# A two-layer LSTM + RNN on one core: one matmul unit of every step moved behind the second layer's recurrent product

## The reference

```python
xW = jnp.einsum('ntd,dk->tnk', x, Wx) + b            # layer 0, 4 gates x 512
def step(carry, xw_t):
    prev_h, prev_c = carry
    a = xw_t + prev_h @ Wh
    i, f, o = sigmoid(a[:, :H]), sigmoid(a[:, H:2*H]), sigmoid(a[:, 2*H:3*H])
    g = tanh(a[:, 3*H:])
    next_c = f * prev_c + i * g
    next_h = o * tanh(next_c)
x = x + hs_of_layer0                                  # then layer 1 on this x
def step1(h, xw_t): return tanh(h @ Wh1 + xw_t)       # xW1 = x @ Wx1 + b1
x = x + hs_of_layer1
```

## Time and profile before

| | before |
|---|---|
| median of 3 runs | 2181.52 us |
| profiled execution, time / span | 2183.09 / 2181.0 us |
| TensorE matmul (PE) busy | 2158.0 us, 99% |
| TensorE weight load (PEld) busy | 1779.9 us, 82% |
| VectorE (DVE) / ScalarE (ACT) busy | 2097.6 us, 96% / 1696.9 us, 78% |
| GpSimd (POOL) busy | 113.9 us, 5% |
| mean granted TensorE clock | 0.998 |

### The profile page before, as it was taken

The page is one execution under the profiler, slowest core; times in us unless marked ns, Lnnn a source line. Parts: engine busy times, 40 slices in busy tenths (PEclk is TensorE's granted clock), DMA queues, the critical chain, the costliest instruction groups (busy, mean ns, idle before and its releaser), DMA issues.

```text
span 2181.0 us, 148256 instructions
## 1 busy us (share of the span) xinstructions
PE 2158.0 (99%) x63856; PEld 1779.9 (82%) x63856; DVE 2097.6 (96%) x11013; ACT 1696.9 (78%) x5916; POOL 113.9 (5%) x165
## 2 busy tenths in 40 slices
PE   7999999999999999999999999999999999999998
PEld 4888888888888888888888888888888888888886
DVE  7999999999999999999999999999999999999998
ACT  5777777777777777777777777777777777777775
POOL 0220000000000000000000000000000000000000
PEclk9999999999999999999999999999999999999999
DMA  5000000000000000000000000000000000000000
GB/s 220 19 14 19 23 24 19 14 19 24 24 18 24 14 19 24 24 19 14 18 24 24 19 24 14 19 24 24 19 14 22 21 24 19 24 14 19 24 14 13
DMA packets 17259, 53.88 MB, mean 25 GB/s; under 512 B 1888, under 2 KB 3040, under 8 KB 15328
## 3 DMA queue, kind: packets, MB, share of 16 engines
q1 hardware_dynamic: 15792, 43.85, 5.6%
q10 hardware_dynamic: 816, 0.56, 0.1%
HBM read 27.62 MB, written 16.78 MB: 20 GB/s over the span
## 4 chain that ended last, share of the span: by engine, by line
PE 97%; DVE 2%; ACT 0%; DMA 0%; issue 0%; ACTq 0%; DVEq 0%
PE in_ps L273 25%; PE rec_first_ps L273 21%; PE rnn_ps L273 20%; PE rec_second_ps L273 20%; PE c_ps L273 11%; DVE largest_slice L503 0%; DMA b_sb<-b 0%; DVE wh_part L555 0%; DVE turned L599 0%; PE in_ps L442 0%; ACT wh_part L802 0%; DVE uv L627 0%; DVE h_parts L653 0%; DVE pre_sb L607 0%; DVE gates_cell L632 0%
## 5 line engine op out<-in xcount | busy, mean ns | idle before, releaser
L273 PE MATMUL rec_first_ps<-wh_part,h_parts 128*32 128x256 f16 x16352 | 544.6, 273 | 2.7 <-DVE h_parts L653 2.2
L273 PE MATMUL rec_second_ps<-wh_part,h_parts 128*32 128x256 f16 x16320 | 543.0, 273 | 2.0 <-DVE wh_part L555 2.0
L273 PEld LDWEIGHTS rec_second_ps<-wh_part,h_parts 128*32 128x32 f16 x16320 | 453.0, 97 | 2.4 <-ACT rec_second_ps L813 2.2
L273 PEld LDWEIGHTS rec_first_ps<-wh_part,h_parts 128*32 128x32 f16 x16352 | 380.0, 95 | 83.9 <-issue 7.4
L273 PE MATMUL in_ps<-wx_sums,x_sums 128*32 128x256 f32 x5760 | 379.7, 379 | 0.0
L838 ACT ACTIVATE gates_cell<-gate_ps,unscale 128x128 f32<-128x128 f32 x511 | 187.6, 367 | 208.6 <-DVE gate_ps L607 208.5
L273 PE MATMUL rnn_ps<-wh_parts,h_parts 128*32 128x256 f16 x8096 | 318.0, 273 | 4.7 <-DVE h_parts L692 4.7
L273 PE MATMUL rnn_ps<-wx_sb,y 128*32 128x128 f32 x8192 | 321.3, 273 | 0.4 <-ACT rnn_ps L825 0.4
L273 PEld LDWEIGHTS rnn_ps<-wx_sb,y 128*32 128x32 f32 x8192 | 252.3, 110 | 80.2 <-ACT rnn_ps L825 0.9
L825 ACT ACTIVATE rnn_ps<-rnn_ps,mask_scaled 128x256 f32<-128x256 f32 x506 | 225.2, 445 | 76.8 <-DVE turned L669 61.7
L273 PEld LDWEIGHTS in_ps<-wx_sums,x_sums 128*32 128x32 f32 x5760 | 195.7, 110 | 92.8
(11 more groups left out here) (116 smaller groups left out, 3386.5 us busy)
## 6 DMA issues: line engine op xcount, KB each, us to landing
yT<-y SPq DMA_DIRECT2D x64, 256.0 KB, 2.4
x_sb<-xT SPq DMA_DIRECT2D x31, 512.0 KB, 4.1
wh_sb<-wh SPq DMA_DIRECT2D x5, 1024.0 KB, 10.3
wx_sb<-wx SPq DMA_DIRECT2D x5, 1024.0 KB, 17.9
b_sb<-b ACTq DMA_DIRECT2D x1, 256.0 KB, 6.0
x_sb<-xT ACTq DMA_DIRECT2D x1, 256.0 KB, 17.8
x_sb<-xT SPq DMA_DIRECT2D x1, 256.0 KB, 21.8
b_sb<-b SPq DMA_DIRECT2D x1, 64.0 KB, 21.4
```

The costliest lines, as they stand in the source:

```text
L273: last = nc.tensor.matmul(out[QUAD * q:QUAD * (q + 1)], states, weights(q), start=False, stop=True, tile_position=(0, QUAD * q), skip_grou ...
```

## The change

The last unit of each step is taken out of its place between `recurrent0` and `input1` and issued at the end of the step, behind `recurrent1`. Its `slot_done` goes with it. Steps without `units` (t below 27) are as before.

```diff
-            def units(g, first, end):
+            def units(g, first, end, last_of_slot):
...
-                last.then_inc(slot_done, 1)
+                if last_of_slot:
+                    last.then_inc(slot_done, 1)
...
                         elif g >= PLAIN:
-                            units(g, UNITS_OF_PART[part], UNITS_OF_PART[part + 1])
+                            units(g, UNITS_OF_PART[part], UNITS_OF_PART[part + 1] - 1, False)
...
                     recurrent1(s)
                     if STEPS - 1 <= t < STEPS + LAG - 1:
                         keep_busy(in0_ps[0], BUSY_GROUPS[t - STEPS + 1])
+                if t < SLOTS:
+                    g, part = divmod(t + 5, SPAN)
+                    if g >= PLAIN:
+                        units(g, UNITS_OF_PART[part + 1] - 1, UNITS_OF_PART[part + 1], True)
```

## The result

| | before | after |
|---|---|---|
| median, 6 runs each | 2181.83 us | 2217.66 us |
| ratio, with 95% interval | | 1.0159 (1.0149 to 1.017) |
| span of the profiled execution | 2181.0 us | 2215.8 us |
| PE / DVE / ACT busy | 2158.0 / 2097.6 / 1696.9 | 2190.7 / 2116.0 / 1695.6 us |
| mean granted TensorE clock | 0.998 | 1.0 |

Forecast were 2205.5 us, 24 more than before; measured are 35.8 more. Lines behind line 368 have moved down by up to 5: L653 is now L658, L692 is L697, L813 is L818, L615 is L620, L787 is L792, L599 is L604.

The account below looks back on a forecast made before the run. TensorE's work (4.13 us) and the loop through VectorE (4.15) were taken to bound each step together. The terms 19.2 + 3.6 + 1.2 = 24 us gave 2205.5 us; likeliest range 2196 to 2222, 8-in-10 range 2192 to 2236.

Parts of the forecast that it names:

- Both engines stand at the limit, so any lateness shows: Per step, TensorE's work (4.13 us) and the loop through VectorE (4.15) are nearly equal; lateness on either shows in full.
- A wait at `recurrent1` of 0.05 behind L692, 4.19 a step: TensorE reaches `recurrent1` earlier and waits for L692: 0.04 over 4.15 in 480 steps, 19.2 us.
- The 0.14 that I kept as a far bound: Gap from L653 to `rec_first_ps`; if it held at `recurrent1`, 0.13 a step, 62 us.
- ScalarE's first seed at R + 0.25: R is the step's start at `rec_first_ps`; ScalarE's first L813 waits for the moved unit and starts 0.55 us later.
- `rec_second_ps` just fits: Seeded by R + 0.68 to 0.71, load at R + 0.77: cost 0; rival of late seeds 2253 us, chance 0.15.
- Part 1, 0 to 0.07, taken 0.03: Units needing ScalarE's L787 start 0.03 to 0.12 late, so `recurrent1` is late: 0.03 in 120 steps, 3.6 us.
- Part 0, 0.01: ScalarE's gates start up to 0.26 late, mostly taken up before L692 and L653: 0.01 x 120, 1.2 us.
- Parts 2 and 3: 0: ScalarE has longer idle times ahead of the gates there, so its later start costs 0.
- the likeliest case's range: 2196 to 2222 us, for 14 to 41 us added; the case has chance 0.70.
- the wide range: 2192 to 2236 us, to hold 8 times in 10; top: half of ScalarE's rival price or the way's far bound.
- the 48: Price of the rival that ScalarE's queue pays: 0.1 us in 480 steps, 2253 us; chance 0.15.
- Clock: Rival: TensorE's pauses in each step lower its clock; one step in ten at half clock, 198 us, 2404; chance 0.01.

Follow-up runs that it names:

- f6: The kernel before, but the first matmul of `recurrent0` no longer makes its redundant wait for `seed0_done[0]` (t = 5 to 507); 2170.51 us, ratio 0.9943.
- e2: The changed kernel, but the last unit is moved behind `recurrent1` in parts 2 and 3 alone; 2192.52 us, ratio 1.0045 to before.
- e3: The changed kernel, but ScalarE waits for the moved unit only where it reads it, part 2 keeping the early wait; 2205.84 us, ratio 1.0108 to before.
- e8: As e3, but part 1 issues its first unit last and part 2's early wait for `slot_done` goes too; 2200.32 us, ratio 1.0084 to before.
- f4: The changed kernel, but the last two units of each step stand behind `recurrent1` instead of one; 2409.39 us, ratio 1.1038 to before.
- f9: e8 with the same redundant `seed0_done[0]` wait removed as in f6; 2196.62 us, ratio 1.0058 to before.
- f5: The kernel before with every unit in its old place, but `slot_done` signalled later, by one of `recurrent1`'s last four matmuls; 2197.06 us, ratio 1.0061.
- e1: The changed kernel, but each step's last unit stands behind `input1` and ahead of `recurrent1`; 2181.29 us, ratio 0.9997 to before.

## Why the prediction was right, and what it mis-sized

- *Both engines stand at the limit, so any lateness shows.* Right. Steps are 4.15 before, and f6 shows that the loop through L653 held them 0.02 above TensorE's own 4.13.
- *A wait at `recurrent1` of 0.05 behind L692, 4.19 a step.* Right in kind and place. In every kernel in which TensorE waits there the median is 0.05 (after in parts 0, 2 and 3, e2, e3, e8, f4, f9); the step is 4.180, so 0.03 a step (15 us) rather than 0.04 (19), and the 0.01 taken for weights that could not be loaded ahead did not come. e8 isolates it: 14 us by its medians, 18 by its time. The 0.14 that I kept as a far bound belongs to a first matmul whose load waits behind a separate semaphore instruction, which this wait does not have: f6 takes that instruction away, and its load comes 0.06 us sooner behind VectorE.
- *ScalarE's first seed at R + 0.25.* Right: 0.25 in part 0, 0.27 in part 2.
- *`rec_second_ps` just fits.* Right; this rival did not come: in parts 0 and 3 the second L604 starts 1.97 to 1.98 into the step (median), as L599 did in before (1.98).
- *Part 1, 0 to 0.07, taken 0.03.* The range held, the value was too low: 0.057 over parts 0 and 3 (7 us instead of 3.6), because the way from L792 to the units is 0.10 where 0.05 to 0.14 was allowed. e3 shows it: with the copies early, the extra is gone.
- *Part 0, 0.01.* It is 0.
- *Parts 2 and 3: 0.* This is the step that failed. Part 3 is 0. In part 2 I looked only at ScalarE's idle time ahead of the gates, and not at who waits for the seed itself: L615 on VectorE does, and it lies in the loop that sets the step. Part 2 pays 0.078 over parts 0 and 3, 9 us; e3 against e8 shows it (0.061 a group, and gone when the early wait is gone), and f5 has it without the move.
- The sum by terms: 15 + 7 + 9 = 31 us by the medians, against 24 forecast. Some 4 us more are in longer steps that I had no term for. That 2217.66 still lies in the likeliest case's range, 2196 to 2222, is in part luck: its high end has room for a wait of 0.06 a step and for 0.03 in part 0, which did not come, and none for part 2, which did. The far end of the wide range, 2236, does not follow from the prices named for it either: half of the 48 gives 2229.5, the far bound of 62 gives 2243.5.
- *Clock.* It did not fall: 1.0 (2.4 GHz) in the profiled execution and 0.998 to 1.0 in the five others, though TensorE pauses in every step; in f4, with a pause of 0.3 us a step, it was 0.999.

## What to carry to other kernels

In a loop where two engines are both full, put behind a waiting instruction nothing that could have stood ahead of it: the work in front of a wait is its cover. f4 shows the price, the whole of the moved work once the cover is gone, while e1 shows that moving it up to the wait is free. When a semaphore is signalled later, list everyone who waits for it and then everyone who waits for those, on every engine; and look for waits that an earlier wait of the same engine has already answered: leaving one out gave 0.6% where the loop through that wait set the step (f6), and nothing in the medians where it did not (f9).

## What the runs showed of the hardware

- From VectorE's end to a weight load that waits for one semaphore were 0.05 us by the medians (`recurrent1` in after, e2, e3, e8, f4 and f9; `rec_first_ps` in f6 and f9).
- Where the same place waits for two semaphores, the trace of before has a separate semaphore instruction on TensorE: L653 ends at 1205.76, that instruction starts at 1205.80 and takes 0.05, the load starts at 1205.87 and the matmul at 1205.90. The load thus comes 0.12 behind VectorE's end; with one wait left (f6) the separate instruction is gone and the load comes 0.05 behind.
- From ScalarE's end to the instruction that waited for it were 0.13 us on VectorE (the seed and the addition into `c_ps`, part 2 of after, e3, f4 and f5) and 0.10 us on TensorE (the copy and the units, part 1 of after, f4 and f5). Both instructions wait for more than one semaphore.
- A wait of TensorE of 0.05 us between matmuls is in no list of waits, because the modelled end of the matmuls before covers it. Starts must be compared.
